# Paged attention on one core: value pages gathered in two indirect transfers per batch instead of four

## What is computed

```python
B, S, HK, HQ, D = 32, 32, 8, 32, 128
PAGES, PSIZE, NPP = 64, 32, 16                       # 16 pages of 32 tokens per batch
L = NPP * PSIZE                                      # 512 cached tokens
kc = k_cache[block_table].reshape(B, L, HK, D)
vc = v_cache[block_table].reshape(B, L, HK, D)
k_all = concatenate([kc, k], axis=1)                 # 512 cached + 32 new tokens
v_all = concatenate([vc, v], axis=1)
valid = concatenate([arange(L)[None] < cache_seqlens[:, None], ones((B, S))], axis=1)
scores = einsum('bqhd,bkhd->bhqk', q, repeat(k_all, 4, axis=2)) * SCALE
probs = softmax(where(valid[:, None, None], scores, -1e30), axis=-1)
o = einsum('bhqk,bkhd->bqhd', probs, repeat(v_all, 4, axis=2))
```

## Time and profile before

| | us |
|---|---|
| device time, median of 3 runs | 1694.57 (1693.58 to 1695.39) |
| device time of the profiled execution | 1689.82 |
| its span, first to last instruction | 1687.6 |
| granted TensorE clock, mean over the span | 0.995 of full speed |
| value gathers: indirect DMAs, bytes | 128, 67.12 MB |
| DMA bytes in all | 290.69 MB |

### The profile page before, as it was taken

The page is one execution under the profiler, slowest core; times in us unless marked ns, Lnnn a source line. Parts: engine busy times, 40 slices in busy tenths (PEclk is TensorE's granted clock), DMA queues, the critical chain, the costliest instruction groups (busy, mean ns, idle before and its releaser), DMA issues. The chain is left out here.

```text
span 1687.6 us, 34168 instructions
## 1 busy us (share of the span) xinstructions
PE 1619.2 (96%) x10792; PEld 1404.1 (83%) x10792; DVE 1104.5 (65%) x2942; ACT 943.1 (56%) x2392; POOL 369.9 (22%) x370
## 2 busy tenths in 40 slices
PE   2899999999999999999979999999999999999998
PEld 2787888888888788888869999999999999977777
DVE  8405543454436657777768888888888888864443
ACT  3224323232222266766669989998899888822221
POOL 1000000000000246656532332223222322122210
PEclk9999999999999999999979999999999999999999
DMA  6621121110110433443578889988998898594301
GB/s 231 206 91 52 65 69 68 68 44 24 68 63 26 162 107 107 134 134 106 156 268 277 282 297 300 305 287 286 304 302 295 273 301 299 184 325 140 122 12 50
DMA packets 239311, 290.69 MB, mean 172 GB/s; under 512 B 18682, under 2 KB 182938, under 8 KB 239258
## 3 DMA queue, kind: packets, MB, share of 16 engines
q1 hardware_dynamic: 220826, 222.89, 39.8%
q0 software_dynamic: 18432, 67.12, 12.3%
HBM read 237.43 MB, written 50.41 MB: 171 GB/s over the span
## 5 line engine op out<-in xcount | busy, mean ns | idle before, releaser
L1591 PE MATMUL p_val<-probs_t,vals 128*128 128x128 f32 x2048 | 271.7, 276 | 1.7 <-DMA vals<-in_v_pages,rows_now 1.7
L1591 PEld LDWEIGHTS p_val<-probs_t,vals 128*128 128x128 f32 x2048 | 249.3, 192 | 2.0 <-DMA vals<-in_v_pages,rows_now 2.0
L1501 DVE CUSTOM_DVE_ANT_0 probs<-p_score,mask 128x544 f32<-128x544 f32 x256 | 184.3, 720 | 80.2 <-issue 77.6
L1406 ACT ACTIVATE probs<-probs,low 128x544 f32<-128x544 f32 x256 | 190.6, 745 | 0.3 <-DVE low L1501 0.3
L1060 POOL TENSOR_TENSOR w_lo<-w_raw,w_hi 128x512 fp32r<-128x512 f32 x44 | 57.7, 1316 | 548.4 <-DVE w_hi L1098 531.9
L1414 ACT ACTIVATE probs_t<-p_turn 128x512 f32<-128x512 f32 x256 | 149.5, 584 | 50.6 <-PE p_turn L1570 46.6
L450 PE MATMUL p_score<-wo_hi,q_hi 128*128 128x288 f32 x448 | 153.4, 342 | 11.9 <-DVE low L1501 11.3
L1490 DVE TENSOR_TENSOR wo_lo<-keys,wo_hi 128x544 fp32r<-128x544 f32 x224 | 161.7, 722 | 0.7 <-issue 0.7
L450 PE MATMUL p_tile<-w_hi,y_hi 128*128 128x512 f32 x384 | 156.9, 409 | 2.4 <-PEq L463 2.4
L1570 PE MATMUL p_turn<-cst,probs 128*128 128x128 f32 x1024 | 154.8, 274 | 3.2 <-issue 1.5
L1401 ACT ACTIVATE wo_hi<-keys 128x544 fp32r<-128x544 f32 x224 | 146.1, 652 | 17.6 <-PE p_score L452 12.9
(11 more groups left out here) (216 smaller groups left out, 3604.4 us busy)
## 6 DMA issues: line engine op xcount, KB each, us to landing
keys<-in_k_pages SPq DMA_DIRECT2D x512, 128.0 KB
qk_new<-x_res SPq DMA_DIRECT2D x80, 256.0 KB, 2.3
x_res<-qk_new SPq DMA_DIRECT2D x32, 512.0 KB
o_new<-x_res SPq DMA_DIRECT2D x32, 512.0 KB
w_raw<-in_w_vkq_t SPq DMA_DIRECT2D x12, 1024.0 KB, 5.6
w_raw<-in_w_qkv_t SPq DMA_DIRECT2D x10, 1024.0 KB, 8.2
toep<-kpad SPq DMA_DIRECT2D x32, 256.0 KB, 4.9
w_raw<-in_w_dense_t SPq DMA_DIRECT2D x8, 1024.0 KB, 5.3
```

Of the source, the lines that this page charges most:

```text
L1406: nc.scalar.activation(probs[:, i % 8, :], probs[:, i % 8, :], ACT.Exp, bias=low[:, i % 4:i % 4 + 1], scale=-1.0, accum_out=total[:, i % 4 ...
L1501: v.tensor_tensor_reduce(out=probs[:, i % 8, :], in0=score_at(i % 2, slice(0, KEYS)), in1=mask[:, i // HK, :], scale=1.0, scalar=3e38, op0 ...
L1591: mm = pe.matmul(p_val[:, h, half * P:(half + 1) * P], vals[:, slot, c, k * D:(k + 1) * D], probs_t[:, i % 2, c, :], start=(c == 0 and hal ...
```

## The change

Each index now names two consecutive tokens: `v_flat` has half as many rows, of 8 KB, and two gathers (`GATHERS`) per batch bring the same 512 tokens. Partition p of gather g holds the tokens 256g + 2p and 256g + 2p + 1, one after the other. To match, transposed block n takes every second column of `probs`: columns 256(n//2) + n%2, step 2. The values product reads its block at the new place, still 128 floats in a row. The indices are made in another way: the table of pages is multiplied with a mask of 0 and 1 (16 new columns of `cst`) that leaves each partition its own page of each eight, summed over groups of eight, and multiplied by 16 with the position in the page, 0 to 15, added (1 new column). Queues, waits and the interleaving stay; counts in the waits follow.

```diff
+RUN = 2
+GATHERS = CACHE // (P * RUN)
...
+    per_page = PSIZE // RUN
+    c[:, C_RUNPAGE:C_RUNPAGE + NPP] = np.arange(NPP)[None, :] % (P // per_page) == (p // per_page)[:, None]
+    c[:, C_RUNPOS] = p % per_page
...
-        for q in range(4):
-            at = slice(S * q, S * q + S)
-            v.tensor_scalar(self.rows[at, :, :], self.pages_f[at, :].rearrange("p (b n q) -> p q b n", b=B, q=4)[:, q], float(PSIZE),
-                            cst[at, C_SPOS:C_SPOS + 1], ALU.mult, ALU.add).then_inc(self.rows_ready, 1)
+        pages = self.pages_f[:, :].rearrange("p (b n) -> p b n", b=B)
+        v.tensor_tensor(pages, pages, bc(cst[:, C_RUNPAGE:C_RUNPAGE + NPP], 1, [P, B, NPP]), ALU.mult).then_inc(self.pages_ready, 1)
+        v.wait_ge(self.pages_ready, 3)
+        v.tensor_reduce(self.rows_f[:, :, :], self.pages_f[:, :].rearrange("p (b g n) -> p b g n", b=B, g=GATHERS), X, ALU.add).then_inc(self.pages_ready, 1)
+        v.wait_ge(self.pages_ready, 4)
+        v.tensor_scalar(self.rows[:, :, :], self.rows_f[:, :, :], float(PSIZE // RUN), cst[:, C_RUNPOS:C_RUNPOS + 1],
+                        ALU.mult, ALU.add).then_inc(self.rows_ready, 1)
...
-            pool.wait_ge(tables.rows_ready, 4)
+            pool.wait_ge(tables.rows_ready, 1)
...
-        vals = sb("vals", [P, 2, NPP // 4, HK * D])
+        vals = sb("vals", [P, 2, GATHERS, RUN * HK * D])
...
-        VALS = 16 * (NPP // 4)
+        VALS = 16 * GATHERS
...
-            v_flat = v_pages.rearrange("o t n -> (o t) n")
+            v_flat = v_pages.rearrange("o (t r) n -> (o t) (r n)", r=RUN)
...
-                    for n in range(NPP // 4):
+                    for n in range(GATHERS):
                         gather(vals[:, slot, n, :], rows_now[:, slot, n:n + 1], v_flat, vals_gathered[slot])
...
-                    mm = pe.transpose(p_turn[:, n, :], probs[:, i % 8, n * P:(n + 1) * P], ident)
+                    mm = pe.transpose(p_turn[:, n, :], probs[:, i % 8, n // RUN * P * RUN + n % RUN:(n // RUN + 1) * P * RUN:RUN], ident)
...
-                    mm = pe.matmul(p_val[:, h, half * P:(half + 1) * P], vals[:, slot, c, k * D:(k + 1) * D], probs_t[:, i % 2, c, :],
+                    mm = pe.matmul(p_val[:, h, half * P:(half + 1) * P], vals[:, slot, c // RUN, c % RUN * HK * D + k * D:c % RUN * HK * D + (k + 1) * D], probs_t[:, i % 2, c, :],
```

More of the change, by code:

```diff
@@ L73 @@
 C_PART = C_KEYPOS + KEYS
-C_COLS = C_PART + 1
+C_RUNPAGE = C_PART + 1
+C_RUNPOS = C_RUNPAGE + NPP
+C_COLS = C_RUNPOS + 1
 def constants():
@@ L854, in __init__ @@
         self.len_f = sb("len4_f", [P, B])
-        self.rows = sb("rows", [P, B, NPP // 4], I32)
-        self.rows_now = sb("rows_now", [P, 2, NPP // 4], I32)
+        self.rows = sb("rows", [P, B, GATHERS], I32)
+        self.rows_f = sb("rows_f", [P, B, GATHERS])
+        self.rows_now = sb("rows_now", [P, 2, GATHERS], I32)
         self.keys_0 = sb("keys_0", [P, NPP + 1, HK, S])
```

## The result

| | before | after |
|---|---|---|
| device time, median (range) of 4 runs each | 1694.98 (1693.58 to 1697.72) us | 1680.16 (1679.14 to 1680.43) us |
| profiled execution, its span | 1689.82, 1687.6 us | 1680.06, 1678.2 us |

The account below looks back on a forecast made before the run. PE was taken to bound the kernel. All terms were zero except the start's -1.1 and +1.8 us; their sum, +0.7, on the median of 1694.57 gave 1695.3 us, range 1690.4 to 1699.4.

Parts of the forecast that it names:

- The gathers in the steady part: nothing: Steady paged attention: 64 fewer indirect DMAs save 72 us of GpSimd's time, but GpSimd waits for PE, so 0.
- The transposes: nothing, if the load stays short: PE's 1024 transposes: the column step lengthens at most the weight load, hidden up to 192 ns; taken as 0.
- rival 2: At the 1024 transposes, each ns of load beyond 192 ns costs 1024 ns; up to 113 us, 1808 us; chance 0.11.
- The 3 ns of spacing: Transposes and value products on PE: their spacings differ by 3 ns, bounding the hidden load's cost at 3 us.
- The start: Start of the paged attention: two opposing terms, -1.1 us and +1.8 us, sum to +0.7 us.
- Term (a): Start of the stage: doubled gathers fill DMA room, so all queued behind lands up to 1.1 us sooner; -1.1 us.
- rival 3: Key pages queue behind doubled rows: 30 us per us beyond 9 us late, or 1699.3 us at the start; chance 0.06.
- Term (b): Start: batch 0's values land sooner, PE waits longer for batch 1's keys, slow clock follows; +1.8 us, else 0.
- The values product: PE's product with the values: its 128 floats stay contiguous, only at another offset; nothing.
- the indices: Making the indices on VectorE: 1.7 us instead of 1.4, hidden by its wait for ScalarE's sine; nothing.
- Rival 1: The start is recovered whole: both waits and the slow stretch go, -4.2 us, 1690.4 us; chance 0.09.
- rival 4: An 8 KB row goes out as two of 4 KB; GpSimd's time per gather doubles, 1694.6 us; chance 0.04.

Follow-up runs that it names:

- before_again: The kernel before, unchanged, run again on a chip where before takes 1667.90 us: 1668.01 us.
- strided_only: The kernel before with its transposes taking every second column, four gathers kept: 1677.33 us, ratio 1.0057.
- gather_per_head_again: The kernel before, its second, third and fourth gather each waiting until one more head's values are through, where before takes 1693.91 us: 1668.14 us, ratio 0.9851.
- paired_read: The change, with VectorE's mask step reading every second PSUM column, even tokens first, so transposes load 128 neighbouring columns: 1669.92 us, ratio 0.9854.
- two_and_two: The kernel before, its third gather waiting until two more heads' values are through, giving two close pairs: 1675.07 us.
- late_values: The kernel before with gathers one head apart, but batch 1's four waiting together for batch 0's first head's values: 1667.88 us.
- late_spread: late_values with batch 1's four gathers one head apart as well: 1665.95 us, ratio 0.9854.

## Why the prediction was wrong

**"The gathers in the steady part: nothing"** is the step that failed by most. It asked who waits for a gather's data and how busy GpSimd is, and stopped there. On the chip of the result the four gathers cost 548.43 - 526.27 = 22.2 us in the profiled run (27 us between the medians of before on S and Q chips; 25.8 us came back on one S chip when the four were set a head apart) by delaying PE's reports. The sign was to be read, though not in the totals (VectorE's 77.6 us before the mask and ScalarE's 46.6 us are 44.4 and 17.1 where nothing stalls) but in the single waits: 30 times VectorE is idle for over 1 us, 1.6 us on average, once per batch and beside a fourth gather. And PE was idle for 13.8 us in the earlier trace rows, which I let pass as 558 of 572; in the same window of before_again it is idle for 0.6.

**"The transposes: nothing, if the load stays short"** failed by its condition. The limit was right: hidden up to the 192 ns of a value product's load. The load came out at 206 ns, and rival 2's rule, 1024 ns for each ns beyond it, gives 14 x 1.024 = 14.3 us; measured are 9.8 us over 29 batches (strided_only), 0.34 each, some 11 us in all. The 3 ns of spacing that bounded this case were read too small as well: the two rows differ by 4 to 5 ns, and the spacing then grew by some 11 ns a transpose (9.8 us over 29 x 32). One head of the change, to set against the earlier trace rows:

```profile
1099.30 0.65 PE L1581 MATMUL p_turn<-cst,probs 128*128 128x128 f32 x4
```

Four transposes take 0.65 instead of 0.60 us. I had given any cost over 3.4 us a chance of 0.11, with one price for all of it, 113 us, and left it out of the range. The measurement also decides between the two halves of the rule of the Trainium skill (SBUF — State Buffer, Door 1: The DMA port swizzle): two hits per 16-byte line, which a step of two floats has, were not enough for full rate here; that each crossing costs agrees in direction.

**The start: +0.7 us forecast, +2.13 measured.** Term (a), the DMA room filled, -1.1 us, was wrong in sign: the keys of batch 1 came 24.29 us after the stage's first product instead of 22.81, because batch 1's values stood before them: its gathers were issued at 863.37 and 864.66 us, among the first key pages, and in the kernel before from 866.30 to 870.11. SyncE's row for their 16 pages, to set against 13.08 us from 863.21 in the kernel before:

```profile
862.76 14.99 SPq L887 DMA_DIRECT2D keys<-in_k_pages  x16
```

This is rival 3 in its small form, at the start only; in the steady part the pages never came late. Term (b), a longer wait for keys and a slow clock behind it, came about, by another road: the wait for values stayed (1.60 us), the clock behind it did not fall, and PE reached the keys early by that. Of the +2.13 us the keys' later landing is 1.48, and the slow clock behind the wait most of the other 0.65 (the product there took 1.99 us instead of 1.18). Windows of the change, where the clock was slow in the earlier trace rows and behind the 3.37 us wait:

```profile
873.00:876.50 3.50, 3.50 (x32) 3.50 (x31) 2.06 (x8) 2.07 (x5) 0.00 (x0) 1.00 1.00 388
884.00:886.00 2.00, 2.00 (x8) 1.47 (x7) 1.95 (x6) 2.00 (x5) 0.00 (x0) 0.50 1.06 291
```

**The rest.** The values product (276 and 275 ns) and the indices stood as forecast. Rival 1 did not come; rival 4 is out: 64 transfers took 61.9 us, 968 ns each, and the packets of that queue went from 18432 to 9216. The sum by measured terms, for the chip of the result: -22.2 + 0.6 for the stalls and +9.8 for the load make -11.8 us in 29 batches (measured -11.7), +2.1 is the start and +0.2 the rest, -9.4 us of span. That the sum fits proves nothing: its first three terms are differences along one chain of four profiles (before on S, before and strided_only on Q, the change on S) and must add up to the difference of the ends. What bears them out are pairs within one kind of chip: gather_per_head_again has 21.4 us less than before in its steady part on S, and the change 10.0 us more than paired_read, which has its gathers without its load. On a Q chip the stalls are nil and the change is slower by what is left, 9.8 + 2.1 and 0.5 behind batch 31, 12.4 us (12.9 between medians; the two profiled executions differ by 3.4 us more ahead of batch 0, which the medians do not show and no term explains). My forecast of no difference was thus wrong by two terms of opposite sign, each several times what I allowed for, and the sign of their sum depends on the chip.

**Open.** Why S chips stall and Q chips do not, by what path close gathers hold up PE's reports, and how the delay grows with their number (0.4 to 0.6 us behind a pair in two_and_two, 1.2 behind three, 1.6 behind four). Each chip gave the same answer whenever it was met, one of each kind twice, but nothing here shows what differs in them. That late_values lost its gain to the four close gathers rests on late_spread alone.

## What to carry to other kernels

Ask of an instruction not only who waits for its result, but what else runs late while it is under way: two engines that resume at the same moment, long after the work they wait for has ended, point to a third thing, and its cost shows as idle time with no releaser. Space indirect transfers over the work they overlap: one head apart that cost nothing on either kind of chip and gave as much as halving them, while two heads apart they came too late and cost 26 us. When an access pattern must be permuted, try it at each reader and writer: here the same permutation cost 11 us in the weight load, 36 us in VectorE's write and nothing in its read of PSUM.

## What the runs showed of the hardware

- One kernel, before, took 1668 us on two chips, 1691 to 1695 on three others and 1695 on that of the result; the change took 1680 on both kinds. A ratio of two kernels from one chip (0.991) turned round on another (1.007).
- On the slower kind, four indirect transfers whose starts lie 1.2 to 1.8 us apart delay VectorE and ScalarE in taking up what PE has finished, by 1.6 and 1.2 us at the fourth; three 1.4 to 1.6 us apart by 1.2 us, in the one batch that has them; with 2.1 us and more between starts nothing is late. The bytes do not matter (1 KB rows stall as 4 KB rows do), and the transfers themselves last the same (1122 ns on average in before, 1129 in before_again).
- A weight load of 128x128 f32 takes 141 ns with neighbouring columns, 206 ns with every second.
- VectorE's mask step over 544 columns takes 720 ns with neighbours or with a read of every second or fourth column in PSUM, 1109 ns when it writes alternately to places 272 columns apart.
